# Turning the base weights on VectorE and ScalarE instead of TensorE

## The reference

```python
y     = einsum('bct,bcd->bdt', x, cond_weights[condition])     # 64 x 64 x 1024
base  = einsum('bsi,oi->bso', y, W_org)                        # 1024 x 1024 weights
q     = einsum('bi,ki->bk', y.mean(axis=1), Wq)
coeffs = softmax(einsum('bk,ek->be', q, lora_keys) / sqrt(128))
h     = einsum('bsi,eir->bser', y, lora_down)
delta = einsum('be,bser,ero->bso', coeffs, h, lora_up)
out   = x + base + delta
```

## Time and profile before

| | |
|---|---|
| median of three runs | 722.35 us |
| profiled execution, whole | 723.07 us |
| its span, first to last instruction | 721.3 us |
| TensorE busy | 705.7 us, 98% |
| VectorE busy | 494.8 us, 69% |
| ScalarE busy | 241.7 us, 34% |
| GpSimd busy | 122.7 us, 17% |
| data moved | 138.61 MB, 192 GB/s |

### The profile page before, as it was taken

The page is one execution under the profiler, slowest core; times in us unless marked ns, Lnnn a source line. Parts: engine busy times, 40 slices in busy tenths (PEclk is TensorE's granted clock), DMA queues, the critical chain, the costliest instruction groups (busy, mean ns, idle before and its releaser), DMA issues.

```text
span 721.3 us, 10640 instructions
## 1 busy us (share of the span) xinstructions
PE 705.7 (98%) x3385; PEld 591.5 (82%) x3385; DVE 494.8 (69%) x808; ACT 241.7 (34%) x466; POOL 122.7 (17%) x110
## 2 busy tenths in 40 slices
PE   5999999999999999999999999999999999999997
PEld 5877888888888888888888877888888888888876
DVE  3889466566575674674666898676767777677774
ACT  4347244244353362441543732112222222111220
POOL 1600000000000000000000023333233332333350
PEclk9999999999999999999999999999999999999999
DMA  8887584672763753532452746666677666666732
GB/s 249 235 248 224 168 233 177 179 237 103 219 213 126 230 164 119 162 136 60 132 189 81 284 164 182 226 220 233 234 233 233 219 234 219 220 208 215 270 124 89
DMA packets 100890, 138.61 MB, mean 192 GB/s; under 512 B 18778, under 2 KB 69986, under 8 KB 98018
## 3 DMA queue, kind: packets, MB, share of 16 engines
q1 hardware_dynamic: 100496, 137.85, 59.8%
q10 hardware_dynamic: 338, 0.07, 0.0%
HBM read 82.32 MB, written 55.57 MB: 191 GB/s over the span
## 4 chain that ended last, share of the span: by engine, by line
PE 88%; DVE 5%; issue 3%; DMA 2%; SPq 1%; ACT 1%; DVEq 0%; POOL 0%; ACTq 0%
PE x_ps L1355 22%; PE w_ps L1355 17%; PE x_ps L1292 11%; PE h_ps L1258 11%; PE x_ps L1258 11%; PE w_ps L1292 8%; PE y_ps L1233 7%; PE w_ps L1343 1%; DMA down_raw<-in_L_ffn_lora_down_dram 1%; DVE tb_l L801 1%; DVE blk L804 1%; SPq L309 1%; DVE up_raw L801 1%; DVE ysum L816 1%; DVE tu_l L801 0%
## 5 line engine op out<-in xcount | busy, mean ns | idle before, releaser
L523 POOL TENSOR_TENSOR blk<-blk,blkx 128x512 f32<-128x512 f32 x60 | 93.3, 1557 | 276.0 <-DMA blkx<-in_x_dram 161.0
L804 DVE TENSOR_TENSOR blk<-w_ps,blk 128x512 f32<-128x512 f32 x96 | 66.0, 689 | 66.4 <-PE w_ps L1292 32.1
L1355 PE MATMUL x_ps<-tb_h,ba_h 128*128 128x512 f32 x256 | 100.1, 391 | 0.8 <-DVE ba_l L801 0.4
L1355 PE MATMUL x_ps<-tb_l,ba_h 128*128 128x512 f32 x256 | 99.7, 389 | 0.0
L1355 PE MATMUL x_ps<-tb_h,ba_l 128*128 128x512 f32 x256 | 99.7, 389 | 0.0
L561 ACT ACTIVATE ba_h<-bs 128x512 fp32r<-128x512 f32 x64 | 38.1, 626 | 125.5 <-DVE bs L801 125.5
L1355 PE MATMUL w_ps<-tb_h,ba_h 128*128 128x512 f32 x192 | 74.9, 390 | 0.0
L1355 PE MATMUL w_ps<-tb_l,ba_h 128*128 128x512 f32 x192 | 74.8, 389 | 0.0
L1355 PE MATMUL w_ps<-tb_h,ba_l 128*128 128x512 f32 x192 | 74.7, 389 | 0.0
L804 DVE TENSOR_TENSOR blk<-x_ps,blk 128x512 f32<-128x512 f32 x64 | 42.5, 683 | 35.7 <-PE x_ps L1355 35.7
L816 DVE TENSOR_REDUCE ysum<-y_full 128x8 f32<-128x512 f32 x64 | 41.6, 680 | 36.2 <-ACT y_full L561 36.2
(11 more groups left out here) (97 smaller groups left out, 1384.0 us busy)
## 6 DMA issues: line engine op xcount, KB each, us to landing
x_sb<-in_x_dram SPq DMA_DIRECT2D x32, 512.0 KB, 4.4
y_dram<-y_full SPq DMA_DIRECT2D x64, 256.0 KB, 2.9
yb<-y_dram SPq DMA_DIRECT2D x32, 512.0 KB, 7.3
out_dram<-blk SPq DMA_DIRECT2D x64, 256.0 KB, 3.8
blkx<-in_x_dram SPq DMA_DIRECT2D x30, 512.0 KB, 7.2
r_dram<-blk SPq DMA_DIRECT2D x56, 256.0 KB, 2.4
blk<-r_dram SPq DMA_DIRECT2D x14, 1024.0 KB, 6.7
t_dram<-st SPq DMA_DIRECT2D x16, 448.0 KB, 3.8
```

Source lines behind the costliest of these rows:

```text
L523: pool.tensor_tensor(blk[p % 3][:, b, :], blk[p % 3][:, b, :], blkx[:, h, n, :], ALU.add).then_inc(x_added, 1)
L804: nc.vector.tensor_tensor(dst, a, b, ALU.add).then_inc(done, 1)
L1355: mm = nc.tensor.matmul(bank, ba[s][n][:, k, :], tb[w][n][:, k, :], start=(first and k == 0 and i == 0), stop=(k == 3 and i == 2), skip_gr ...
```

## The change

Weights are no longer turned by TensorE. VectorE transposes the whole piece in one instruction, which turns each block of 32 by 32 in place. ScalarE then moves blocks to their partitions: 16 copies a step, each from 32 partitions to 32 partitions, of 8 groups of 32 elements (`spread_w(s, 0)` and `spread_w(s, 1)`, eight each). The four blocks lie in slots 0 to 3 of `st[i]`, and VectorE makes the four sums in SBUF. The target of the transpose, `wt[i]`, is the second half of `st[i]`, so slots of the operands are numbered anew (`SLOT`). `up_7` no longer waits for the readers of `w_ps`.

The lists change too. `turn_w(2q-2)` stands on VectorE where `sum_w(2q-2)` was, `turn_w(2q-1)` behind `scale_h(q, 1)` and ahead of `sum_y(n+2)`, and `sum_w(2q-2)` behind `sum_y(n+3)`. On SP `load_w(2q-1)` now stands at m = 1, `store_t(2q-2)` at m = 2, and `load_w(2q)` and `store_t(2q-1)` at m = 3.

```diff
+SLOT = {P1: 0, P2: 1, P7: 2, P3: 3, P5: 4, P6: 5, P4: 6}
+QB = 32
+        wt = [at(f"wt_{i}", 182272 + 8192 * i + 4096, [P, 8, P]) for i in range(2)]
...
-                             t_dram[n].rearrange("p k f -> p (k f)")).then_inc(t_loaded[n], 16)
+                             t_dram[SLOT[n]].rearrange("p k f -> p (k f)")).then_inc(t_loaded[n], 16)
...
                     if q < NQ - 2:
                         load_x(t + 4 + m)
                         load_cw(t + 4 + m)
-                    if 1 <= q <= 4 and m % 2 == 0:
-                        step = 2 * (q - 1) + m // 2
-                        store_t(step)
-                        if step < 7:
-                            load_w(step + 1)
+                    if 1 <= q <= 4 and m == 1:
+                        load_w(2 * q - 1)
+                    if 1 <= q <= 4 and m == 2:
+                        store_t(2 * q - 2)
+                    if 1 <= q <= 4 and m == 3:
+                        if q < 4:
+                            load_w(2 * q)
+                        store_t(2 * q - 1)
...
-            def take_w(s):
-                q, i = s // 2 + 1, s % 2
+            def spread_w(s, half):
+                i = s % 2
                 act.wait_ge(w_turned, s + 1)
-                act.wait_ge(blk_stored[i], 64 * q + 32 * (q - 1))
-                copy(st[i][:, P1:P2 + 1, :, :].rearrange("p n k f -> p (n k f)"), w_ps[:, 0, :], w_copied)
-                copy(st[i][:, P3, :, :].rearrange("p k f -> p (k f)"), w_ps[:, 1, 2 * P:4 * P], w_copied)
+                for b in (2 * half, 2 * half + 1):
+                    for f in range(4):
+                        copy(st[i][QB * f:QB * (f + 1), 0:4, :, QB * b:QB * (b + 1)].rearrange("p n k f -> p (n k) f"),
+                             wt[i][QB * b:QB * (b + 1), :, QB * f:QB * (f + 1)], w_copied)
...
                 if 1 <= q <= 4:
-                    take_w(2 * q - 2)
+                    spread_w(2 * q - 2, 0)
...                                                      # exps(q), copy_y(n+2), copy_y(n+3)
+                if 1 <= q <= 4:
+                    spread_w(2 * q - 2, 1)
+                    spread_w(2 * q - 1, 0)
                 hi_block(j0, P1, 0, 0)
                 hi_sum(j0, P7, 2)
...                                                      # copy_y(n+4), copy_y(n+5)
                 if 1 <= q <= 4:
-                    take_w(2 * q - 1)
+                    spread_w(2 * q - 1, 1)
...
+            def turn_w(s):
+                q, i = s // 2 + 1, s % 2
+                dve.wait_ge(w_loaded, 32 * (s + 1))
+                dve.wait_ge(blk_stored[i], 64 * q + 32 * (q - 1))
+                nc.vector.transpose(wt[i][:, :, :].rearrange("p n f -> p (n f)"),
+                                    w_raw[:, :, :, :].rearrange("p h a f -> p (h a f)")).then_inc(w_turned, 1)
+
             def sum_w(s):
                 i = s % 2
-                b12 = w_ps[:, 1, 0:2 * P].rearrange("p (k f) -> p k f", k=2)
-                dve.wait_ge(w_turned, s + 1)
-                dve.wait_ge(w_copied, 2 * s + 2)
-                sub(st[i][:, P5, :, :], b12, st[i][:, P1, :, :], t_sum)
-                sub(st[i][:, P7, :, :], st[i][:, P3, :, :], b12, t_sum)
+                def slot(n):
+                    return st[i][:, SLOT[n], :, :]
+                dve.wait_ge(w_copied, 16 * (s + 1))
+                sub(slot(P5), slot(P7), slot(P1), t_sum)
                 dve.wait_ge(t_sum, 4 * s + 1)
...
                 if 1 <= q <= 4:
-                    sum_w(2 * q - 2)
+                    turn_w(2 * q - 2)
                 softmax_first(q)
                 softmax_last(q)
                 scale_h(q, 0)
                 scale_h(q, 1)
+                if 1 <= q <= 4:
+                    turn_w(2 * q - 1)
                 if more:
                     sum_y(n + 2)
                     sum_y(n + 3)
+                if 1 <= q <= 4:
+                    sum_w(2 * q - 2)
                 sum_3(j0)
...
-                if j >= 2 and j % 2 == 0:
-                    pe.wait_ge(w_copied, 4 * min(j // 2, 4))
-                    pe.wait_ge(t_sum, 8 * min(j // 2, 4) - 2)
                 up_product(j, P7, w_ps[:, 1, :], True, 5)
...
-            def turn_w(s):                                # TensorE's, with its eight transposes
...
-                        if 1 <= q <= 4 and r == 0:
-                            turn_w(2 * (q - 1) + a)
```

More of the change, by code:

```diff
@@ L953, in split_t @@
                 sub(tb[1][n][:, part, :], tb_f[n][:, part, :], tb[0][n][:, part, :], tb_lo)
+            def turn_w(s):
[4 more added lines that the diff above has]
+                                    w_raw[:, :, :, :].rearrange("p h a f -> p (h a f)")).then_inc(w_turned, 1)
             def sum_w(s):
                 i = s % 2
-                b12 = w_ps[:, 1, 0:2 * P].rearrange("p (k f) -> p k f", k=2)
-                dve.wait_ge(w_turned, s + 1)
-                dve.wait_ge(w_copied, 2 * s + 2)
-                sub(st[i][:, P5, :, :], b12, st[i][:, P1, :, :], t_sum)
-                sub(st[i][:, P7, :, :], st[i][:, P3, :, :], b12, t_sum)
+                def slot(n):
+                    return st[i][:, SLOT[n], :, :]
+                dve.wait_ge(w_copied, 16 * (s + 1))
+                sub(slot(P5), slot(P7), slot(P1), t_sum)
                 dve.wait_ge(t_sum, 4 * s + 1)
-                sub(st[i][:, P6, :, :], st[i][:, P3, :, :], st[i][:, P5, :, :], t_sum)
+                sub(slot(P7), slot(P3), slot(P7), t_sum)
+                sub(slot(P6), slot(P3), slot(P5), t_sum)
                 dve.wait_ge(t_sum, 4 * s + 3)
-                sub(st[i][:, P4, :, :], st[i][:, P2, :, :], st[i][:, P6, :, :], t_sum)
+                sub(slot(P4), slot(P2), slot(P6), t_sum)
             def b_sum_1(p):
@@ L1330, in up_4 @@
                 up_product(j, P4, w_ps[:, 1, :], False, 7)
-            def turn_w(s):
[L1333 to L1345, removed]
             def base_product(p, n, bank, first, built):
```

## The result

The changed kernel takes 779.43 us in the median of six runs (777.6 to 780.87); the kernel before took 722.1 beside it. The ratio is 1.0796, interval 1.0778 to 1.0814: 57 us slower. The forecast was 776.

What follows compares the result with a forecast made beforehand. TensorE was taken to bound the kernel, never waiting, so each added wait lengthens it. Stalls less removed transposes gave 49.5 us, the clock 4.4: 53.9 on 723.07 is 777.0, the median 776 us; range 755 to 800.

Steps and rivals of the forecast that it cites:

- (c): Weights of step 2q-1 land 5.3 us after their load starts, at 26.2; bounds 3.6 and 5.7.
- (d): VectorE waits ten microseconds in `turn_w(2q-1)` for weights; transposing ends at 27.4, ScalarE's eight copies at 30.0.
- (e): TensorE wants `make_y(n+6)` at 27.3, but ScalarE's `copy_y(n+4)` runs 31.0 to 31.6: first stall 4.3 us.
- (f): Last eight copies end at 34.6, VectorE's list at 40.5; TensorE ready for `up_2` at 36.1: second stall 4.4.
- (g): `store_t(2q-1)` lands at 51.4 and `take_r(j1,0)` ends at 52.0, so `up_6(j1)` waits: third stall 6.1.
- (h): The quarter ends at 62.9 against 49.87: +13.0 in three quarters, +10.5 in q = 4, sum 49.5 us.
- Cover of the first half: ScalarE's idle 5.49 us before the exponentials hides step 2q-2's first eight copies (2.6), ending near 12.5.
- The late load and the late store: On SP, `load_w(2q-1)` stands behind y, x and cw, `store_t(2q-1)` behind `load_w(2q)`: stalls of 4.3, 4.4, 6.1.
- The clock: TensorE slows after the 6.1 us waits before `up_6(j1)`: 1.5 for each of three, bounds 0 and 2.9; 4.4 us.
- The one where only the store bites (733): Weights are there when VectorE asks (16.3); late `store_t` alone costs 3.4 per quarter, 0.9 in q = 4; chance 0.09.
- The one with the slow clock behind every third wait and copies that don't overlap (790): TensorE's clock costs 2.9 in each of four quarters, ScalarE's copies 0.41 apart cost 1.6 per quarter; chance 0.20.
- The faster one (715): VectorE's and ScalarE's free shares cover all: -7.0, if weights land before 16.3 and the store before 36.6; chance 0.05.

Runs made afterwards that it cites:

- the replanned kernel: The changed kernel's same new instructions, with weight loads, stores, transposes and copies placed anew in the lists; 714.27 us, ratio 0.9905.
- The load-early kernel: The changed kernel with `load_w(2q-1)` at m = 0 behind `load_cw` instead of m = 1, stores unmoved; 754.15 us, ratio 1.0442.
- the kernel with both edits: The changed kernel with `load_w(2q-1)` at m = 0 and `store_t(2q-1)` right behind the y stores at m = 3; 728.20 us, ratio 1.0088.
- the kernel with the filler: The changed kernel with 16 useless matmuls on TensorE just ahead of `up_6(j1)` in quarters 1 to 4; 775.38 us, ratio 1.0744.

## Why the prediction was right

By its steps, for q = 2, counted from 136.90 (us):

| step | forecast | measured |
|---|---|---|
| (a) `copy_y(n+3)` starts | 14.8 | 14.8 |
| (b) `load_w(2q-1)` starts | 19.6 | 19.2 |
| (c) weights landed | 26.2 | 24.8 |
| (d) transposed; eight copies done | 27.4; 30.0 | 26.1; 29.6 |
| (e) `make_y(n+6)` starts | 31.6 | 31.0 |
| (f) last copies done; `up_2(j0)` starts | 34.6; 40.5 | 34.8; 41.1 |
| (g) `store_t(2q-1)` starts, landed | 47.0; 51.4 | 45.7; 51.7 |
| (g) `up_6(j1)` starts | 52.0 | 52.5 |
| (h) quarter ends | 62.9 | 64.9 |

- **What bounds.** Right: TensorE had been busy throughout, and its waits lengthened the run. Counted as the forecast counts them, from when TensorE would be ready at full clock, the stalls of q = 2 are 3.6, 5.6 and 6.0 against 4.3, 4.4 and 6.1. The removed transposes gave their 7.0: in the replanned kernel quarters 1 to 4 last 48.1 instead of 49.87; its medians differ by 7.5.
- **Cover of the first half.** Right, but for less than was thought: the exponentials came 0.35 us after the copies, as eight of these take 3.5 and not 2.6.
- **The late load and the late store.** Shown by taking each away alone and together, and by the order alone, which costs 33 us in the old kernel.
- **Sizes.** Five terms were off, and off in both directions. Weights landed 1.4 earlier: y, x and cw took SP 4.4 and not 4.8, the two loads were issued 0.6 us apart and not 1.3, and the second landed after 5.0 and not 5.3. Eight copies took 0.9 more, twice; `load_w(2q)` held SP for 1.25 and not 2.5; `store_t` landed after 5.4 and not after the median 3.8. They leave 0.5 at `up_6(j1)`. That they cancel so nearly is luck, and so are the 1.9 us ahead of quarter 1, which no step foresaw and without which 776 would have been 5 too low.
- **The clock.** Right in kind and too small. The twelve matmuls behind the third wait took 4.53, 4.43, 5.49 and 4.60 us in the four quarters, 8.2 over 4 x 2.72. In q = 3 the twelve behind these took 3.1, another 0.4; the granted clock there is 0.56 over the 7 us from 254.6, against 0.78 over the 7 us from 189.4 in q = 2. Of these 8.6 us 4.4 was in the sum, and q = 4 was wrongly taken at nothing. Without them the quarters grew by 59.4 - 8.6 = 50.8, against 49.5. That a slow TensorE behind the second wait is absorbed showed as well: four products took 7.3 us (177.97 to 185.28) instead of 5.4, and the third wait was 4.1 idle instead of 6.1. The level at the start of the run, from which the price was taken, rests on lengths alone, as the forecast says: the view by windows prints 1.00 for 6 to 13 us, but the trace has no entry of the clock before 12.2.
- **Rivals.** The one where only the store bites (733) did not come about, as VectorE waited 8.5 us for weights. The load-early kernel makes its condition true: the second transpose of q = 2 starts 16.3 into the quarter and waits for nothing. It took 754 all the same, as three blocks of eight copies took 0.9 more each, `up_6(j1)` started at 45.2 instead of 42.4, and the clock cost 2.3 to 2.8 a quarter; that rival had priced itself too low. The one with the slow clock behind every third wait and copies that don't overlap (790) was right in both kinds, and on the clock its 11.6 is nearer to 8.6 than the 4.4 of the forecast. What its copies cost by themselves was not isolated; each eight took 0.9 more, and the shorter issues and the earlier landing made up for that. The faster one (715) is what the replanned kernel is: its weights are there before 16.3, its store has landed at 31.8, before 36.6, and it takes 714.3.

Left open: why an issue of `load_w` takes 0.6 us here and took 1.1 to 1.6 behind `store_t` before (median landing 3.7 against 5.3), and what sets the start of quarter 1.

## What to carry to other kernels

Work moved from a full engine to engines with idle shares brings its whole time only if every list it stands in is followed: the load that feeds it, the store that frees its buffer, and each instruction behind a wait. Here the same instructions cost 57 us or gave 7.5, by where a load, a store and a few copies stood. Before such a move, write down for each buffer when its data lands and when its next writer is wanted; where a DMA queue is one list in order, what stands ahead of a load is part of its latency.

## What the runs showed of the hardware

- ScalarE's copies overlap by 0.1 us where the next one reads and writes from the same first partition as the last: 0.31 apart for 256 elements. With a change of it they are 0.42 to 0.44 apart. The Trainium skill has such a rule for VectorE ("VectorE: DVE Perf Modes", section on two Vector instructions with no wait between them); no run here shows it there.
- VectorE's transpose of 128x1024 f32 in blocks takes 1.24 us, as long as a subtraction of that size.
- Idle times of TensorE of 3.6 to 4.3 us ahead of `up_6(j1)` were followed by 1.7 to 3.2 us lost at the lower clock; with 1.88 and 0.63, in the kernel with both edits, the profiled run's granted clock was 1.000 over the whole span (0.992 to 1.000 in its four runs). The length of the wait alone doesn't settle it: in the kernel with the filler the first waits of q = 2 and q = 3 are 2.14 and 2.07 us at the same place, and the granted clock behind them is 0.51 in the one (165.8 to 169.2) and 1.00 in the other (227.9 to 231.2).
